# Attention of layer 1 in pairs of heads: fills at two places of a slot, their banks emptied early and midway, q and k nine slots ahead, rings of three pairs

## The reference

```python
def _L1_attn_ref(x, W_in, b_in, W_out, b_out):      # called on the layernorm of x; H = 16, KD = VD = 64
    proj = x @ W_in.T + b_in
    q, k, v = ...                                   # each (b, 16, 512, 64)
    q = _rope(q, sin, cos); k = _rope(k, sin, cos)
    att = jnp.einsum('bhqd,bhkd->bhqk', q, k) * scale
    att = jnp.where(mask, att, -inf)                # causal
    att = softmax(att, axis=-1)
    y = jnp.einsum('bhqk,bhkd->bhqd', att, v)
    return y.transpose(0, 2, 1, 3).reshape(b, t, H * VD) @ W_out.T + b_out
```

## Time and profile before

| what | us |
|---|---|
| median of three runs | 2496.54 |
| the profiled execution | 2484.7 |
| its span | 2482.9 |
| TensorE busy | 1913.1 (77%) |
| VectorE busy | 1673.6 (67%) |
| ScalarE busy | 1260.3 (51%) |
| GpSimd busy | 962.3 (39%) |

### The profile page before, as it was taken

How to read it: one execution, slowest core, us unless ns; L and a number is a source line. 1 busy time by engine, 2 the same in 40 slices (tenths; PEclk the granted TensorE clock), 3 DMA queues, 4 the chain that set the end, 5 groups by cost and what they waited for, 6 DMA issues and landing times. The chain is left out here.

```text
span 2482.9 us, 50691 instructions
## 1 busy us (share of the span) xinstructions
PE 1913.1 (77%) x17990; PEld 1270.8 (51%) x17991; DVE 1673.6 (67%) x3654; ACT 1260.3 (51%) x2545; POOL 962.3 (39%) x1103
## 2 busy tenths in 40 slices
PE   2999999998629974767777777777777777729999
PEld 1666666666616641435445454444545445515665
DVE  3888888887824434775756657566565765679998
ACT  1666666666624442654554545556454554524443
POOL 4443444431050014683454434445344453332222
PEclk8999999999559996999999999999999999959999
DMA  6000000000333222231111111111011111010000
GB/s 224 2 2 2 2 2 2 2 2 2 104 131 91 83 66 49 41 65 26 35 27 27 35 27 27 35 27 35 18 35 27 27 35 27 18 35 11 17 17 24
DMA packets 63952, 90.70 MB, mean 37 GB/s; under 512 B 11312, under 2 KB 49360, under 8 KB 63744
## 3 DMA queue, kind: packets, MB, share of 16 engines
q1 hardware_dynamic: 57088, 78.06, 11.5%
q0 software_dynamic: 6656, 9.85, 1.9%
HBM read 35.71 MB, written 18.61 MB: 22 GB/s over the span
## 5 line engine op out<-in xcount | busy, mean ns | idle before, releaser
L969 DVE TENSOR_REDUCE neg_max_sb<-a_bank 128x1 f32<-128x128 f32 (+3 forms) x512 | 221.1, 483 | 339.1 <-PE a_bank L763 339.0
L889 ACT ACTIVATE p_hi_sb<-a_bank 128x384 f16<-128x384 f32 (+1 forms) x384 | 202.1, 529 | 329.2 <-PE a_bank L773 329.2
L457 DVE TENSOR_REDUCE neg_max_sb<-a_bank 128x1 f32<-128x128 f32 (+3 forms) x512 | 235.5, 484 | 88.8 <-PE a_bank L237 85.0
L815 PE MATMUL a_bank<-xnT_sb,w_in_sb 128*128 128x512 f16 x768 | 193.9, 390 | 125.9 <-DVE rope_sb L998 89.8
L976 DVE TENSOR_TENSOR p_lo_sb<-a_bank,p_hi_sb 128x384 f16<-128x384 f32 (+1 forms) x384 | 229.0, 598 | 71.6 <-ACT p_hi_sb L889 63.8
L880 ACT ACTIVATE prob_sb<-a_bank,neg_max_sb 128x128 f32<-128x128 f32 (+3 forms) x512 | 257.3, 535 | 26.8 <-DVE neg_max_sb L969 26.5
L380 ACT ACTIVATE probT_sb<-a_bank 128x512 f32<-128x512 f32 (+1 forms) x384 | 198.8, 527 | 137.6 <-PE a_bank L260 132.8
L1083 POOL TENSOR_TENSOR rope_lo_sb<-rope_sb,rope_hi_sb 128x512 f16<-128x512 f32 x128 | 146.3, 1171 | 310.0 <-ACT rope_hi_sb L916 310.0
L1075 POOL TENSOR_TENSOR t_swapped_sb<-t_swapped_sb,sin_sb 128x512 f32<-128x512 f32 x128 | 166.8, 1303 | 119.3 <-DMA t_swapped_sb<-t_buf_sb 119.2
L773 PE MATMUL a_bank<-ident_f_sb,prob_sb 128*128 128x128 f32 x1280 | 190.0, 291 | 2.5 <-DVE p_lo_sb L976 2.0
L815 PEld LDWEIGHTS a_bank<-xnT_sb,w_in_sb 128*128 128x128 f16 x768 | 67.1, 100 | 201.4 <-DVE rope_sb L998 96.9
(11 more groups left out here) (267 smaller groups left out, 5108.3 us busy)
## 6 DMA issues: line engine op xcount, KB each, us to landing
t_swapped_sb<-t_buf_sb SPq DMA_DIRECT2D x256, 128.0 KB
sorted_rows<-zeros_sb SPq DMA_DIRECT2D x1, 4992.0 KB, 22.2
x_in_sb<-sorted_rows SPq DMA_DIRECT2D x39, 128.0 KB, 2.1
...
```

Source lines behind the costliest of these rows:

```text
L457: last = dve.tensor_reduce(neg_max[:, h % 2, i:i + 1], S[(3 * h + g) % 2][:, off:off + L], AX.X, ALU.max, negate=True)
L815: last = pe.matmul(out, w["in"][:, w_, c, t * 1024 + p * P:t * 1024 + (p + 1) * P], xnT[:, b % 2, x, c, :], start=n == 0, stop=n == len(te ...
L889: act.activation(p_hi[g][:, h % 2, :], PT[h % 2][:, 0:GROUP_COLS[g]], ACT.Copy).then_inc(s_hi, 1)
L969: last = dve.tensor_reduce(neg_max[:, h % 2, i:i + 1], S[h % 2][:, off:off + L], AX.X, ALU.max, negate=True)
```

## The change

Six things change, all in `attention1` and its table.

1. A fill now has a slot and a place. Place 0 is right behind the scores, ahead of the transposes; place 1 is at the end of the slot, where all fills stood. All q and k are at place 0; each slot but one has one fill at place 0, 17 of 24 have one at place 1, and no place has two.
2. Fills at place 0 are taken midway in the same slot: on ScalarE behind the first exponential, on VectorE behind the first `lo`. Fills at place 1 are taken at the very start of the next slot, on VectorE ahead of the row maxima.
3. On ScalarE `hi` now stands behind `exp` of the same head and not ahead of it.
4. `take_out` moves from the start of slot 3p+5 to the end of slot 3p+4, and `normalize` stays at the end of the slot ahead of its xT fill, which are now the slots 8, 10, 11 and 13.
5. q and k of pair p stand at slots 3p-9 and 3p-8 and not at 3p-6 and 3p-5; the steps behind them are one or two slots longer apart: the rotations come 4 and 3 slots behind the fills, the high parts 5 and 4, the low parts 6 and 5. The rings of rotated q and k hold three pairs, those of `t_buf` and `t_sw` two, with a semaphore for each half. So three pairs are prepared ahead of slot 0, and not two.
6. One loop runs over all slots of all batches, with the last slots of a batch beside the first of the next, the newer batch first in each step; the output projections stand at slots 27 to 30 (one in each) and not at 27, 28, 29, 29.

```diff
-AT1 = (tuple(3 * p - 6 for p in range(HEADS // 2)), tuple(3 * p - 5 for p in range(HEADS // 2)),
-       (1, 7, 8, 9), (16, 18, 19, 21), (10, 12, 13, 15), (27, 28, 29, 29), 0)
+AT1 = (tuple(3 * p - 9 for p in range(HEADS // 2)), tuple(3 * p - 8 for p in range(HEADS // 2)),
+       ((0, 1), (2, 0), (8, 0), (10, 1)), ((15, 1), (17, 0), (18, 1), (20, 0)), ((9, 1), (11, 0), (12, 1), (14, 0)),
+       ((7, 1),) + tuple((3 * c + 5, 1) for c in range(1, HEADS // 2)), ((27, 1), (28, 1), (29, 0), (30, 1)))
...
-    LAG_WA, LAG_WV, LAG_VH, LAG_VL = 1, 1, 1, 2
-    LAG_W, LAG_ZH, LAG_ZL = (3, 2), (4, 3), (4, 3)
-    LAG_OUT = LAG_PV + 3
-    AT_Q, AT_K, AT_V1, AT_V0, AT_XT, AT_PROJ, YT_LAG = AT1
+    LAG_VH, LAG_VL = 1, 2
+    LAG_W, LAG_ZH, LAG_ZL = (4, 3), (5, 4), (6, 5)
+    LAG_OUT = LAG_PV + 2
+    AT_Q, AT_K, AT_V1, AT_V0, AT_XT, AT_YT, AT_PROJ = AT1
+    RING = 3
...
-    t_buf = sb("t_buf", [P, 2, T], F32)
-    t_sw = sb("t_swapped", [P, 2, T], F32)
-    rope = sb("rope", [P, 4, T], F32)
+    t_buf = sb("t_buf", [P, 2, 2, T], F32)
+    t_sw = sb("t_swapped", [P, 2, 2, T], F32)
+    rope = sb("rope", [P, 2 * RING, T], F32)
...
@@ TensorE @@
-        def slot(b, k, last):
-            if k < SLOTS_:
-                scores(b, k // 3, k % 3)
-            for a in range(2):
-                if 0 <= k - LAG_T < SLOTS_:
-                    transpose_probs(b, (k - LAG_T) // 3 * 2 + a, (k - LAG_T) % 3)
-            for a in range(2):
-                if 0 <= k - LAG_PV < SLOTS_:
-                    pv(b, (k - LAG_PV) // 3 * 2 + a, (k - LAG_PV) % 3)
-            for kind, ahead, *a in work(k, last):
-                fill(b + ahead, kind, *a)
+        def slot(parts):
+            for b, p, g in groups(parts, 0):
+                scores(b, p, g)
+            for b, *work_ in fills(parts, 0, 0):
+                fill(b, *work_)
+            for b, p, g in groups(parts, LAG_T):
+                for a in range(2):
+                    transpose_probs(b, 2 * p + a, g)
+            for b, p, g in groups(parts, LAG_PV):
+                for a in range(2):
+                    pv(b, 2 * p + a, g)
+            for b, *work_ in fills(parts, 0, 1):
+                fill(b, *work_)
@@ ScalarE @@
+            for b, kind, *c in fills(parts, 1, 1):
+                take(kind, b, *c)
             for a in range(2):
-                if 0 <= k - LAG_HI < SLOTS_:
-                    hi(b, (k - LAG_HI) // 3 * 2 + a, (k - LAG_HI) % 3)
-                if k < SLOTS_:
-                    exp(b, k // 3 * 2 + a, k % 3)
+                for b, p, g in groups(parts, 0):
+                    exp(b, 2 * p + a, g)
+                if a == 0:
+                    for b, kind, *c in fills(parts, 0, 0):
+                        take(kind, b, *c)
+                for b, p, g in groups(parts, LAG_HI):
+                    hi(b, 2 * p + a, g)
@@ VectorE @@
-            p, r = divmod(k - LAG_OUT, 3)
-            if r == 0 and 0 <= p < PAIRS:
-                for a in range(2):
-                    take_out(b, 2 * p + a)
...
+            for b, kind, *c in fills(parts, 1, 1):
+                take(kind, b, *c)
+            for b, p, g in groups(parts, 0):
                 for a in range(2):
+                    row_max(b, 2 * p + a, g)
             for a in range(2):
-                if k < SLOTS_:
-                    row_max(b, k // 3 * 2 + a, k % 3)
-            for a in range(2):
-                if 0 <= k - LAG_LO < SLOTS_:
-                    lo(b, (k - LAG_LO) // 3 * 2 + a, (k - LAG_LO) % 3)
-            for kind, ahead, *a in work(k - LAG_WV, last):
-                take(kind, b + ahead, *a)
+                for b, p, g in groups(parts, LAG_LO):
+                    lo(b, 2 * p + a, g)
+                if a == 0:
+                    for b, kind, *c in fills(parts, 0, 0):
+                        take(kind, b, *c)
+            for b, p, g in groups(parts, LAG_OUT):
+                for a in range(2):
+                    if g == 0:
+                        take_out(b, 2 * p + a)
@@ SyncE @@
-            wait(sp, s_z, 2 * pr)
+            wait(sp, s_z, 2 * (pr - 1))
```

More of the change, by code:

```diff
@@ L686, in attention1, with work @@
     s_wout = sem("out_weights_split")
-    def work(k, last):
+    def work(k, last, place=None):
         out = []
@@ L731, in run @@
         prologue()
-        for b in range(B):
-            last = b == B - 1
-            for k in range(SLOTS_):
-                if b == 0 and besides:
-                    besides(eng, 2 * k)
-                    besides(eng, 2 * k + 1)
-                slot(b, k, last)
-                if b > 0 and k + SLOTS_ < TAIL:
-                    slot(b - 1, k + SLOTS_, False)
-        for k in range(SLOTS_, TAIL):
-            slot(B - 1, k, True)
+        for s in range((B - 1) * SLOTS_ + TAIL):
+            if s < SLOTS_ and besides:
+                besides(eng, 2 * s)
+                besides(eng, 2 * s + 1)
+            slot([(b, s - b * SLOTS_) for b in range(B - 1, -1, -1) if 0 <= s - b * SLOTS_ < TAIL])
     @block.tensor
@@ L848, in prologue @@
                 fill(0, "xT", j)
-            for p in range(2):
+            for p in range(RING):
                 for t in range(2):
@@ L1050, in prologue, with slot @@
             split_out_weights()
[L1052 to L1054 removed]
+        def slot(parts):
+            for b, kind, *c in fills(parts, 1, 1):
+                take(kind, b, *c)
+            for b, p, g in groups(parts, 0):
                 for a in range(2):
[L1056 removed]
+                    row_max(b, 2 * p + a, g)
             for a in range(2):
[L1058 to L1066 removed]
+                for b, p, g in groups(parts, LAG_LO):
[7 more added lines that the diff above has]
+                        take_out(b, 2 * p + a)
+            for b, kind, j in fills(parts, -1, None, "xT"):
+                normalize(b, j)
         run(dve, prologue, slot, besides=aside[1])
@@ L1102, in prologue, with slot @@
                 value_lo(0, 0, j)
-        def slot(b, k, last):
-            for ahead, half, j in of("V", k - LAG_VL, last):
-                value_lo(b + ahead, half, j)
+        def slot(parts):
+            for b, kind, half, j in fills(parts, LAG_VL, None, "V"):
+                value_lo(b, half, j)
             for t in range(2):
-                for ahead, t_, p in of("qk", k - LAG_ZL[t], last):
+                for b, kind, t_, p in fills(parts, LAG_ZL[t], None, "qk"):
                     if t_ == t:
-                        rope_lo(b + ahead, t, p)
-                for ahead, t_, p in of("qk", k - LAG_W[t], last):
+                        rope_lo(b, t, p)
+                for b, kind, t_, p in fills(parts, LAG_W[t], None, "qk"):
                     if t_ == t:
-                        rotate(b + ahead, t, p)
+                        rotate(b, t, p)
         run(pool, prologue, slot, besides=aside[2])
```

75 lines of the change are left out of this document (38 added, 37 removed).

## The result

The changed kernel takes 2374.21 us (median of 4 runs, 2373.12 to 2377.74) against 2494.01 us of the kernel before in the same comparison: a ratio of 0.9523, 95% interval 0.9503 to 0.9543, 119.8 us less. The forecast was 2396 us, with a range of 2322 to 2448. In the profiled executions the span went from 2482.9 to 2373.3 us, 109.6 us less.

The account below looks back on a forecast made before the run. No engine is full; the meeting of in-order engines bounds the stage, with TensorE waiting for banks. Savings of 96 + 7 + 2 - 4 = 101 us from 2484.7 give 2384, plus the median's 11.8 us: 2396, range 2322 to 2448.

Parts of the forecast that it names:

- The chain: VectorE and ScalarE work from row maxima to next scores closes each slot: 4.1 us in class 2, before extras.
- the bank waits: TensorE's waits in front of fills for banks VectorE has not emptied, about 210 of 254 us; forecast to go.
- The yT take: VectorE's place 1 yT take, ahead of row maxima, waits for ScalarE behind two rope_hi; such class 2 slots take 5.6 us.
- Normalize: VectorE, end of slots 8, 10, 11, 13: 2.0 us each, between 1.64 and 2.44 with one GpSimd collision.
- The ends: Outside batches 1 to 6: batch 0 saves 2 us, batch 7 saves 7, the third pair costs 4 at the start.
- The level: Whole kernel: 101 us off the profiled 2484.7 gives 2384; the median's distance of 11.8 us is kept, giving 2396.
- A: Rival: TensorE becomes the bound, slack absorbs VectorE's extras; 2290 us in full, 2345 half way; chance 0.15.
- B: Rival: hand-overs cost 0.3 us a slot more and port waits hit the chain; 141 us a batch, 2442 us; chance 0.18.
- C: Rival: slower, second exponential queued behind the take and first hi, 0.63 us later each slot; 2518 us; chance 0.06.
- D: Rival: no net change, 2496 us, two-fill slots' gains given back in normalize, yT and take_out slots; chance 0.03.
- The signs: Profile marks of a right forecast: fill waits nearly gone, VectorE waiting about 1.2 us a slot ahead of lo, batch about 134 us.

Follow-up runs that it names:

- the GpSimd experiment: The changed kernel with GpSimd's rotation, addition and rope_lo on 8 columns instead of 512, so less than the task: 2315.04 us in one execution.
- a2: The changed kernel with q and k six and five slots ahead, the lags of before and rings of two pairs: 2388.86 us, ratio 0.9572.
- a1: The changed kernel with every fill at place 1, so all are taken at the start of the next slot: 2355.76 us, ratio 0.9447.
- c1: The changed kernel with hi ahead of exp for each head on ScalarE, as before the change: 2400.49 us, ratio 0.9641.
- g1: The kernel before with one edit, VectorE taking the previous slot's fills at the slot's start, ahead of take_out and row maxima: 2418.21 us, ratio 0.972.

## Why the prediction was right, point by point

**The chain.** The forecast was that the loop over row maxima, exponentials and scores takes the place of the bank waits, with 134.1 us a batch. Measured are 133.1 us. By slots (us, forecast / measured in batch 3):

| slots | | | |
|---|---|---|---|
| 0 to 2 | 5.1 / 4.9 | 5.2 / 4.9 | 5.6 / 4.9 |
| 3 to 5 | 5.3 / 5.1 | 6.3 / 6.1 | 5.5 / 5.4 |
| 6 to 8 | 6.5 / 6.2 | 5.8 / 5.7 | 6.8 / 7.2 |
| 9 to 11 | 4.5 / 4.5 | 7.8 / 8.3 | 6.1 / 9.5 |
| 12 to 14 | 4.5 / 4.3 | 7.2 / 7.2 | 5.5 / 5.4 |
| 15 to 17 | 5.1 / 4.9 | 5.2 / 4.9 | 5.6 / 4.9 |
| 18 to 20 | 5.1 / 4.9 | 5.2 / 4.9 | 5.6 / 4.9 |
| 21 to 23 | 4.5 / 4.3 | 5.2 / 4.8 | 4.9 / 4.9 |

The sum is closer than its terms, and that is in part luck: slot 11 takes 3.4 us more than forecast and slots 8 and 10 0.9 us more, the other slots 5.3 us less. Two terms were mis-sized most, with opposite signs.

**The yT take.** Slots 2, 17 and 20 take 4.9 and not 5.6 us. Slot 20 on VectorE's timeline, and then ScalarE's part of it:

```profile
1509.43 1.28 DVE L974 TENSOR_REDUCE neg_max_sb<-a_bank 128x1 f32<-128x512 f32 x2
1511.24 0.56 DVE L981 TENSOR_TENSOR p_lo_sb<-a_bank,p_hi_sb 128x384 f16<-128x384 f32 x1 [0.54 <-ACT p_hi_sb L889]
1511.72 0.68 DVE L1011 SCALAR_TENSOR_TENSOR v_buf_sb<-a_bank,bias_sb 128x512 f32<-128x512 f32 x1
1512.32 0.55 DVE L981 TENSOR_TENSOR p_lo_sb<-a_bank,p_hi_sb 128x384 f16<-128x384 f32 x1
1513.72 0.69 DVE L1017 TENSOR_TENSOR yT_sb<-a_bank,yT_sb 128x512 f16<-128x512 f32 x1 [0.86 <-ACT yT_sb L911]
1514.33 0.81 DVE L974 TENSOR_REDUCE neg_max_sb<-a_bank 128x1 f32<-128x128 f32 x3
```

```profile
1511.10 0.69 ACT L880 ACTIVATE prob_sb<-a_bank,neg_max_sb 128x512 f32<-128x512 f32 x1
1511.67 0.50 ACT L889 ACTIVATE p_hi_sb<-a_bank 128x384 f16<-128x384 f32 x1
1512.04 1.17 ACT L917 ACTIVATE rope_hi_sb<-rope_sb 128x512 f16<-128x512 f32 x2
1513.08 0.61 ACT L911 ACTIVATE yT_sb<-a_bank 128x512 f16<-128x512 f32 x1
```

The mechanism is the forecast one: VectorE's L1017 waits 0.86 us for ScalarE's L911, which stands behind both `rope_hi`, and the next row maxima (1514.33) stand behind it. But ScalarE has nothing to take at place 0 here. No class 2 slot has a q or k at place 0, and a V fill is taken by VectorE alone; I had put the t_buf copy of 0.69 us into these slots. Of the four slots with V at place 0, slots 2, 17 and 20 are 0.7 us shorter by that; slot 8 is not, because of its normalize. Class 1 slots are 0.3 us shorter, since there TensorE has done the fill before ScalarE comes to its copy.

**Normalize.** Slot 11 takes 9.5 and not 6.1 us. All engines, the end of that slot:

```profile
1462.30 1.36 DVE L1031 TENSOR_SCALAR xn_sb<-x_sb_sb,mv_sb,rstd_sb 128x256 f32<-128x256 f32 x1
1462.39 1.12 POOL L1099 TENSOR_TENSOR v_stage_sb<-v_buf_sb,v_stage_sb 128x512 f16<-128x512 f32 x1 [5.77 <-ACT v_stage_sb L923]
1463.47 2.37 POOL L1094 TENSOR_TENSOR rope_lo_sb<-rope_sb,rope_hi_sb 128x512 f16<-128x512 f32 x2
1463.70 1.12 DVE L1035 CAST xn_part_sb<-xn_sb 128x256 f16<-128x256 f32 x1
1464.86 1.26 DVE L1037 TENSOR_TENSOR xn_part_sb<-xn_sb,xn_part_sb 128x256 f16<-128x256 f32 x1
1465.80 1.45 POOL L1084 TENSOR_TENSOR t_swapped_sb<-t_swapped_sb,sin_sb 128x512 f32<-128x512 f32 x1
1466.16 1.38 DVE L1039 TENSOR_TENSOR x_sb_sb<-x_sb_sb,bias_out_sb 128x256 f32<-128x256 f32 x1
1467.40 1.26 POOL L1088 TENSOR_TENSOR rope_sb<-rope_sb,t_swapped_sb 128x512 f32<-128x512 f32 x1
```

The four instructions of a normalize (L1031, L1035, L1037, L1039) take 1.36, 1.12, 1.26 and 1.38 us. Each ends 0.1 to 0.3 us after a GpSimd operation ends: GpSimd runs `value_lo`, two `rope_lo` and the rotations nearly without a pause. Forecast was one such wait of 0.8 us in half of the cases; here are four in one slot, 5.2 us and not 2.0. Slot 8 has part of it too, 3.3 us, while slots 10 and 13 take 1.5 us; together 11.6 us a batch and not the 8.0 of the forecast. The rule of the Trainium skill, SBUF — State Buffer, "SBUF: two separate sides", that the loser on the shared port pair waits out the whole operation of the other, agrees with these rows and with the GpSimd experiment. What was too small is the number of such waits that I took, because I did not lay GpSimd's run, released by `rope_hi`, beside the slot.

**The ends.** Batch 0 was forecast 2 us shorter and is. The start was forecast 4 us longer for the third pair, and is 3.4 us longer. But the kernel with two pairs ahead (a2) is 7.5 us shorter there than the changed one, about what the six GpSimd operations were expected to take, so something else in the change gives some 4 us back; what, no run shows, and this term was right in part by luck. Batch 7 gains 12 and not 7 us; its slots 15 to 22, without a take at place 0, take 3.6 to 4.0 us but for slot 17 with 4.9.

**The level.** The sum was 101 us and the profiled executions differ by 109.6, which is 9 of the 22 us of the miss. The other 13 us are the distance of the median from the profiled execution, 11.8 us before, which I carried over: the changed kernel's median lies 0.9 us below its profiled execution of 2375.09 us. By the record that distance is scatter and belongs to no kernel: the executions of the kernel before ran from 2481.3 to 2506.2 us over all comparisons, and the profiled one, 2484.7 us, is near the fast end.

**The rivals.** A and B both fall: TensorE has a wait for an exponential in most slots (117 in seven batches), and with hand-overs at what the rows said the batch came out at 133 and not at 141 us. C had the second exponential behind a take and the first `hi`. The take there does cost: without it (a1) the kernel is 18 us faster. `hi` there does not: with each `hi` ahead of its `exp` (c1) it is 26 us slower. D falls with the measured time. I excluded that the change does something else than it says; in a sense it does. The early place is not where the gain comes from, it is a loss of 18 us alone, and the longer lead with its rings is a small part, 15 us. What the early take of the banks brings alone is 69 us of 120 (g1).

**The signs.** Those of "right" came but for one: the waits in front of fills for `rope_cos` and V gone, those for yT only down from 24 to 14 us, the longest wait in front of the scores, VectorE waiting 217 us ahead of `lo` (1.3 us a slot), 133 us a batch, and slots 8, 10, 11 and 13 the longest, with 4 and 6 next.
